# A ring of gathered rows, released by SyncE at an exact count of slots in place of a bound

## The chip, the cores and the metric

The kernel runs on one core of a Trainium2 chip. The metric is the device time of one execution in microseconds; where there are several, their median counts.

## The reference

A graph of 2500 nodes (512 features) and 40000 edges, sorted by destination, goes through two layers of attention with 8 heads of 64, and after them through a dense mixing layer, a node MLP and a gated feed-forward network. Only the attention matters here:

```python
for l in range(L):                                   # L = 2
    q, k, v = (x @ Wq[l] + bq[l]), (x @ Wk[l] + bk[l]), (x @ Wv[l] + bv[l])     # (N, H, D) each
    a = (q[dst] * k[src]).sum(-1) * scale
    e = jnp.exp(a - segment_max(a, dst)[dst])
    alpha = e / (segment_sum(e, dst)[dst] + 1e-16)
    agg = segment_sum(alpha[:, :, None] * v[src], dst)
    x = agg + (x @ Ws[l] + bs[l]) + enc
```

## The kernel before

The program is a row of stages, each in a block that ends with a barrier of all engines: ordering of the edges (skipped where they are sorted), `index_edges`, `normalise_project` (projections of the first layer), `edge_attention`, `combine_project` (projections of the second layer), `edge_attention` again, and then the dense stages. There is no scheduler: what stands in an engine's block runs in that order, and semaphores join the engines.

**Tiles and slots.** The edges lie in ET = 313 tiles of 128. The nodes lie in NT = 20 tiles of 128. Since the edges are sorted, an edge tile mostly belongs to one node tile, and where a node tile begins inside an edge tile, that edge tile is worked on twice. One such piece of work is a slot: there are USED = ET + NT - 1 = 332 of them, in the order of the edges. Edge tile t is used for the last time in slot t + (the number of later node tiles begun by then), so at most in slot t + 19.

**`index_edges`** finds out which slot belongs to what, once, for both layers. VectorE counts edges per node tile, gets from it for each node tile its first edge tile (`flo`), its first slot (`cum`) and how much slot and edge tile differ by then (`dshift`, stepwise). It puts such numbers on a diagonal (`diag`) and reduces it, so that they lie one to a partition (`begins`); compares all slot numbers with them (`begun`); and TensorE sums over the partitions by a matmul of 20x336. The results go as integers into `numbers`, 32 partitions each, from which the engines load registers: `tile_of`, `k_arrival`, `v_arrival`. The masks that follow are written to HBM by SyncE (line 443), and the stage ends with their landing.

**`edge_attention`** first computes the scores (k rows), then the softmax, then the aggregation (v rows). Both gathers go through `ring`: 48 buffers of 128x512 f32, all 48 of which serve for v. In the aggregation

- GpSimd issues one gather (indirect DMA) of 128 rows for each edge tile (line 1244). At most four are in flight: before gather n it waits for the landing of gather n - 4 (FLIGHT). It also waits until the buffer is free:

```python
else:
    pool.wait_ge(weighted, t - NV + NT + 1)
pool.sem_inc(started, 1)
gather(n, v_dram, t)
```

  Tile t takes the buffer of tile t - NV (NV = 48), and the count t - NV + NT + 1 is one that holds for it however the node tiles lie: 20 slots more than slot t - NV itself.
- SyncE waits for the landings in order and counts them for VectorE in `v_arrived` (`arrive`, line 1213):

```python
for t in range(ET):
    arrive(ET + t, v_arrived)
```

- VectorE weights the rows of each slot with the attention weights (line 1373, 128x512), which raises `weighted` by one. Before each fourth slot it builds a matrix of ones and zeros (line 1362), copies weights (1365) and loads the arrival numbers of the next four slots into registers (`slot_numbers`). It may be 16 slots ahead of TensorE.
- TensorE sums slot after slot into PSUM, two halves of a row, four f32 matmul records a slot (line 1506). ScalarE writes out each finished node tile (lines 1429 to 1432).

Of the kernel before, what the change touches and what calls it, by code (L numbers as in the profile page):

```python
# [14 lines left out]
P = 128  # L15
# [7 lines left out]
NT = -(-N // P)  # L23
NP = NT * P
LAST = N - (NT - 1) * P
ET = -(-E // P)
# [18 lines left out]
NV = 48  # L45
# [140 lines left out]
def share_edges(nc, mem, T):  # L186

    T["full_at"] = mem.sb("full_at", [P, NT], I32)
    numbers = mem.sb("numbers", [P, SLOTS], I32)
    T["tile_of"], T["k_arrival"], T["v_arrival"] = (numbers[r:r + 32, :] for r in (0, 32, 64))  # L190
    T["local"] = mem.sb("local", [P, SLOTS + U // 2])
    T["disorder"] = mem.sb("disorder", [P, 1], I32)
    T["local_rows"] = nc.dram_tensor("local_rows", (SLOTS, P), BF16).ap()
    T["src"] = mem.sb("src", [P, ET], I32)
    T["mask_rows"] = nc.dram_tensor("mask_rows", (P, MASKS), BF16).ap()
    T["linked"] = mem.sb("linked", [H, 2 * CH, 2 * CH], BF16)
# [145 lines left out]
def index_edges(nc, a, T, ordered, names):  # L342


    with ExitStack() as stack:
# [20 lines left out]
        diag = m.sb("diag", [NT, 2, NT])  # L366
        begins = m.sb("begins", [NT, 2])
        begun = m.sb("begun", [NT, SLOTS])
        step_up = m.sb("step_up", [NT, P])
# [32 lines left out]
        with nc.Block() as block:  # L402
# [46 lines left out]
            def _(vec):  # L449
# [44 lines left out]
                c.then(vec.tensor_tensor(diag[:, 1, :], dshift[0:NT, :], ident, ALU.mult))  # L494
                c.wait()
                c.then(vec.tensor_reduce(begins[:], diag[:], AX.X, ALU.add))
                c.wait()
                c.then(vec.tensor_scalar(begun[:], slot[0:NT, :], begins[:, 0:1], None, ALU.is_ge))
                c.then(vec.tensor_scalar(step_up[:], ones[0:NT, :], begins[:, 1:2], None, ALU.mult))
                c.wait()  # L500
                vec.nop().then_inc(begun_done, 1)
                vec.wait_ge(stepped, 2)
# [4 lines left out]
                for r, first in (("k_arrival", K_FIRST), ("v_arrival", V_FIRST)):  # L507
                    at = slice(32, 64) if first == K_FIRST else slice(64, 96)
                    c.then(vec.tensor_scalar(T[r], etile[at, :], float(ET - 1), float(first), ALU.min, ALU.add))
                c.then(vec.tensor_scalar(up[:], cum[:, 1:NT + 1], 1.0, None, ALU.add))  # L510
                c.wait()
                c.then(vec.tensor_copy(T["full_at"][:], up[:]))
                for k in range(EK):

                    c.then(vec.tensor_scalar(pick[:, k, :], etile[:], -float(P * k), part[:, 0:1], ALU.add,
                                             ALU.is_equal))
# [55 lines left out]
            def _(pe):  # L572
# [10 lines left out]
                pe.matmul(pss[:], step_up[:], begun[:], start=True, stop=True).then_inc(stepped, 1)  # L583
                pe.wait_ge(picked, 1)
# [555 lines left out]

def edge_attention(nc, a, T, layer, k_dram, v_dram, agg_dram, q_space, y_space, scores):


    with ExitStack() as stack:
# [4 lines left out]
        PER_ROWS = 8  # L1149
        ring = m.sb("ring", [P, NV, C])  # L1150
# [50 lines left out]
        agg_out = [m.sem(f"agg_out{b}") for b in range(AB)]  # L1201
        k_arrived, v_arrived = m.sem("k_arrived"), m.sem("v_arrived")
# [5 lines left out]
        with nc.Block() as block:  # L1208
            @block.sync
            def _(sp):  # L1210
# [22 lines left out]
                for t in range(ET):  # L1233
                    arrive(ET + t, v_arrived)

            @block.gpsimd
            def _(pool):
# [17 lines left out]
                for t in range(ET):  # L1255
                    n = ET + t
                    if t < NB:
                        pool.wait_ge(multiplied, min(n - NB + NT + 1, USED))
                    elif t < NV:

                        pool.wait_ge(reduced, BATCHES)
                        pool.wait_ge(reduced_act, BATCHES * (B - V) * H)
                    else:
                        pool.wait_ge(weighted, t - NV + NT + 1)
                    pool.sem_inc(started, 1)
                    gather(n, v_dram, t)
# [1277 lines left out]
```

## Time and profile before

| | |
|---|---|
| median of three runs | 3196.03 us |
| lowest and highest | 3192.73 and 3197.9 us |
| the profiled execution's own time | 3192.62 us |
| its span, from the first to the last instruction | 3190.5 us |
| TensorE matmul / weight load busy | 2531.2 / 1883.2 us |
| VectorE / ScalarE / GpSimd busy | 2171.0 / 1150.6 / 1644.5 us |
| mean granted TensorE clock | 0.899 of full speed |

The profiled execution is a run of its own, 0.1% below the median of the three. The busy times are sums over stages with different limits, so a share of the span says little on what a change in one stage is worth. The aggregation of the first layer runs from about 803 to 1170 us of the span, that of the second from about 1884 to 2252 us.

### The profile page before, as it was taken

The page shows a single profiled execution, that of the slowest core. Times are in us where ns is not written, and L with a number is a line of the kernel's source. Part 1 is how long each engine was busy: PE and PEld are TensorE (multiplying, and loading weights), DVE is VectorE, ACT ScalarE, POOL GpSimd, SP SyncE. Part 2 cuts the span into 40 slices and gives each one's busy share as a digit, 9 for nine tenths or more (in the row PEclk, how much of TensorE's full clock was granted, in tenths as well). Part 3 has the DMA queues.
Part 4 walks back from the last instruction along what each step waited for, and adds up shares of the span by engine and source line. Part 5 has one row for each costly group of instructions (what it writes and reads, how often), then busy time and mean ns, then how long its engine had stood idle before and what let it go on. Part 6 is the DMA issues. An engine that isn't in the chain of part 4 may idle for free. (4 is left out here: it accounts for less than half of the span.)

```text
span 3190.5 us, 46149 instructions
## 1 busy us (share of the span) xinstructions
PE 2531.2 (79%) x9872; PEld 1883.2 (59%) x9872; DVE 2171.0 (68%) x3512; ACT 1150.6 (36%) x4306; POOL 1644.5 (52%) x1559
## 2 busy tenths in 40 slices
PE   1999766664988879996666759888785999699998
PEld 1788444433776557874444448666564767477776
DVE  5766588888967765437888888777465454566665
ACT  0555466664000020016666610000353322155554
POOL 0101577777677741117777767777122443355555
PEclk9999787877999989997877769999887999899999
DMA  2565577776677774437777757777542332251111
GB/s 102 169 209 181 172 209 206 209 210 189 194 210 222 222 238 139 139 116 211 209 211 210 211 170 212 224 220 219 170 144 78 109 131 92 88 174 40 39 42 36
DMA packets 215857, 524.52 MB, mean 164 GB/s; under 512 B 30652, under 2 KB 48424, under 8 KB 215238
## 3 DMA queue, kind: packets, MB, share of 16 engines
q0 software_dynamic: 100160, 328.28, 35.5%
q1 hardware_dynamic: 98182, 161.91, 15.1%
q10 hardware_dynamic: 17280, 31.63, 2.6%
q8 instruction: 94, 1.54, 0.2%
q14 instruction: 141, 1.16, 0.1%
HBM read 439.83 MB, written 81.88 MB: 164 GB/s over the span
## 5 line engine op out<-in xcount | busy, mean ns | idle before, releaser
L1244 POOL DMA_INDIRECT edge_ring<-v_rows,edges_src x626 | 616.4, 985 | 237.3 <-issue 133.2
L1244 POOL DMA_INDIRECT edge_ring<-k_rows,edges_src x626 | 592.0, 946 | 252.9 <-issue 147.8
L1506 PE MATMUL edge_psA<-layer_q_space 128*128 128x256 f32 (+1 forms) x2656 | 639.0, 395 | 99.0 <-DVE layer_q_space L1373 90.8
L1506 PEld LDWEIGHTS edge_psA<-layer_q_space 128*128 128x128 f32 x2656 | 499.9, 194 | 237.8 <-issue 167.5
L1373 DVE TENSOR_TENSOR layer_q_space<-edge_ring,edge_psQ 128x512 f32<-128x512 f32 x664 | 431.9, 689 | 173.3 <-SPq L1213 136.8
L108 PE MATMUL proj_psP<-proj_w,proj_xT 128*128 128x512 f32 x1920 | 465.9, 400 | 7.0 <-DVE proj_xT L846 4.0
L1460 PE MATMUL edge_psQ<-layer_q_space,edge_hotT 128*128 x888 | 336.7, 527 | 132.8 <-ACT edge_hotT L1398 87.0
L1385 ACT ACTIVATE edge_ring<-edge_ring 128x64 f32<-128x64 f32 x1328 | 319.9, 242 | 286.2 <-DVE edge_ring L1296 286.2
L108 PEld LDWEIGHTS proj_psP<-proj_w,proj_xT 128*128 128x128 f32 x1920 | 359.7, 190 | 91.3 <-DVE proj_xT L846 4.4
L1296 DVE TENSOR_TENSOR edge_ring<-edge_psQ,edge_ring 128x512 f32<-128x512 f32 x444 | 286.4, 684 | 102.2 <-ACT edge_ring L1385 69.9
L1460 PEld LDWEIGHTS edge_psQ<-layer_q_space,edge_hotT 128*128 128x128 f32 x888 | 218.3, 257 | 218.6 <-issue 172.4
L1277 DVE TENSOR_REDUCE layer_scores<-edge_ring 128x24 f32<-128x1536 f32 x166 | 289.4, 1743 | 0.0
L2415 POOL TENSOR_TENSOR ffn_sums<-ffn_sums 128x512 f32<-128x512 f32 x110 | 173.0, 1573 | 199.2 <-DVE ffn_sums L2445 199.2
L1429 ACT COPY layer_q_space<-edge_psA 128x256 f32<-128x256 f32 x80 | 26.1, 379 | 688.2 <-PE edge_psA L1506 688.2
L1385 ACT ACTIVATION_READ_ACCUMULATOR edge_ring<-edge_ring 128x1 f32 x1328 | 247.6, 186 | 0.0
L1460 PE MATMUL edge_psA<-layer_q_space,edge_hotT 128*128 x440 | 169.2, 520 | 62.2 <-ACT edge_hotT L1398 39.1
L1296 DVE TENSOR_TENSOR edge_ring<-edge_psA,edge_ring 128x512 f32<-128x512 f32 x220 | 142.5, 684 | 49.1 <-ACT edge_ring L1385 37.4
L1460 PEld LDWEIGHTS edge_psA<-layer_q_space,edge_hotT 128*128 128x128 f32 x440 | 106.5, 254 | 105.2 <-issue 82.8
L2384 ACT ACTIVATE ffn_sums<-ffn_psP,kept_means 128x512 f32<-128x512 f32 x220 | 139.3, 684 | 79.7 <-PE ffn_psP L2339 78.5
L2445 DVE SCALAR_TENSOR_TENSOR ffn_sums<-ffn_psP,kept_means,ffn_sums 128x512 f32<-128x512 f32 x220 | 154.6, 743 | 17.1 <-PE ffn_psP L2339 16.6
L108 PE MATMUL ffn_psO<-ffn_downT,ffn_hT 128*128 128x512 f32 x660 | 153.2, 391 | 0.0
L1445 PE MATMUL edge_psA<-layer_y_space,edge_ones 1*128 1x512 bf16 x166 | 76.3, 462 | 90.1 <-DMA layer_y_space<-local_rows 90.0
(295 smaller groups left out, 3442.3 us busy)
## 6 DMA issues: line engine op xcount, KB each, us to landing
agg_rows<-layer_q_space ACTq DMA_DIRECT2D x40, 260.0 KB, 4.0
base_rows<-proj_enc SPq DMA_DIRECT2D x40, 256.0 KB, 2.1
k_rows<-proj_out ACTq DMA_DIRECT2D x40, 256.0 KB, 3.4
v_rows<-proj_out ACTq DMA_DIRECT2D x40, 256.0 KB, 2.5
edge_ring<-k_rows,edges_src POOLq DMA_INDIRECT x626, 3.7
edge_ring<-v_rows,edges_src POOLq DMA_INDIRECT x626, 3.7
ffn_downT<-down_rows SPq DMA_DIRECT2D x11, 512.0 KB, 10.2
proj_agg<-agg_rows SPq DMA_DIRECT2D x20, 260.0 KB, 3.1
```

The costliest lines, as they stand in the source:

```text
L108: last = pe.matmul(out, left[i], right[j], start=start and n == 0, stop=stop and n == 2)
L1244: pool.indirect_dma_start(ring[:, buffer[n], :], None, rows, bass.IndirectOffsetOnAxis(ap=T["src"][:, t:t + 1], axis=0)).then_inc(landed[b ...
L1277: vec.tensor_reduce(scores[:, j * B * H:(j * B + V) * H], prod[:, at:at + V, :].rearrange("p i (h d) -> p i h d", h=H), AX.X, ALU.add).the ...
L1296: vec.tensor_tensor(prod[:, s % (2 * B), :], psQ[s % QB][:], one(ring[:, bass.ds(arrived[i] % NB, 1), :]), ALU.mult).then_inc(multiplied, 1)
L1373: vec.tensor_tensor(wv[:, s % R, 0:C].rearrange("p (h d) -> p h d", h=H), ring[:, bass.ds(arrived[s % B] % NV, 1), :].rearrange("p o (h d) ...
L1385: act.activation(at, at, ACT.Copy, accum_out=scores[:, s * H + head:s * H + head + 1]).then_inc(reduced_act, 1)
L1445: pe.matmul(psB[j % 2], ones[:], rows_at[k % 2][0:1, at * P:at * P + B * P], start=True, stop=True).then_inc(spread, 1)
L1460: last = pe.matmul(psQ[(j * B + i) % QB][:], hotT[j % 2][:, i * P:(i + 1) * P], one(qp[:, k, bass.ds(tiles[i], 1), :]), start=(k == 1), st ...
L1506: last = pe.matmul(psA[:, bass.ds(d % 2, 1), e, 0:hi - lo].rearrange("p o w -> p (o w)"), hot[:, s % R, :], wv[:, s % R, lo:hi], start=Fal ...
L2384: act.activation(sums[:, f % 2, j, k, :], psP[k][:], ACT.Copy, scale=W["means"][:, j, f * KC + k:f * KC + k + 1]).then_inc(scaled, 1)
L2415: pool.tensor_tensor(sums[:, f % 2, j, 0, :], sums[:, f % 2, j, 0, :], sums[:, f % 2, j, 1, :], ALU.add).then_inc(summed, 1)
L2445: vec.scalar_tensor_tensor(out=half, in0=psP[k][:], scalar=W["means"][:, j, f * KC + k:f * KC + k + 1], in1=half, op0=ALU.mult, op1=ALU.ad ...
```

## The change

`index_edges` works out a fourth row of numbers, `slots_of`: for each edge tile the number of slots that must be done before its buffer is free. It needs a third diagonal (of `flo`), a second comparison (`opened`: which node tiles have begun by edge tile t), a third matmul and two more operations on VectorE. SyncE loads these numbers into registers, four at a time, waits on `weighted` for the exact count and raises `released` by one for each tile. It does so six tiles ahead of its own loop (AHEAD), between the signals to VectorE. GpSimd waits on `released` in place of `weighted`.

```diff
@@ share_edges
-    T["tile_of"], T["k_arrival"], T["v_arrival"] = (numbers[r:r + 32, :] for r in (0, 32, 64))
+    T["tile_of"], T["k_arrival"], T["v_arrival"], T["slots_of"] = (numbers[r:r + 32, :] for r in (0, 32, 64, 96))
@@ index_edges
-        diag = m.sb("diag", [NT, 2, NT])
-        begins = m.sb("begins", [NT, 2])
+        diag = m.sb("diag", [NT, 3, NT])
+        begins = m.sb("begins", [NT, 3])
...
+                c.then(vec.tensor_tensor(diag[:, 2, :], flo[0:NT, :], ident, ALU.mult))
...
+                c.then(vec.tensor_scalar(opened[:], slot[0:NT, :], begins[:, 2:3], None, ALU.is_ge))
...
-                vec.wait_ge(stepped, 2)
+                vec.wait_ge(stepped, 3)
...
+                c.then(vec.tensor_tensor(past[:], slot[:], pst[0][:, 0:SLOTS], ALU.subtract))
...
+                c.then(vec.tensor_scalar(T["slots_of"], past[96:P, :], 1.0, float(USED), ALU.add, ALU.min))
...
+                pe.matmul(pst[0][:, 0:SLOTS], step_up[:], opened[:], start=True, stop=True).then_inc(stepped, 1)
@@ new function
+def last_slots(nc, engine, T, block, n):
+
+    return nc.values_load_multi_w_load_instructions(T["slots_of"][0:1, bass.ds(block, n)], engines=[engine.engine],
+                                                    min_val=1, max_val=USED)[1]
@@ edge_attention
+        AHEAD = 6
...
+        released = m.sem("released")
...
                 for t in range(ET):
+                    r = t + AHEAD - NV
+                    if 0 <= r < ET - NV:
+                        if r % B == 0:
+                            ends_of = last_slots(nc, sp, T, r, B)
+                        sp.wait_ge(weighted, ends_of[r % B])
+                        sp.sem_inc(released, 1)
                     arrive(ET + t, v_arrived)
...
-                        pool.wait_ge(weighted, t - NV + NT + 1)
+                        pool.wait_ge(released, t - NV + 1)
```

The first place is VectorE in the indexing. Before, from the second diagonal product to the last small integer conversion:

```order
L494 TENSOR_TENSOR index_diag<-index_dshift,kept_ident 20x20
L496 TENSOR_REDUCE index_begins<-index_diag 20x2
L498 TENSOR_SCALAR index_begun<-index_slot,index_begins 20x336
L499 TENSOR_SCALAR index_step_up<-index_ones,index_begins 20x128
L503 TENSOR_SCALAR index_tile_of<-index_psd 128x336
L504 TENSOR_TENSOR index_etile<-index_slot,index_pss 128x336
L506 CAST edges_numbers<-index_tile_of 32x336
L509 TENSOR_SCALAR edges_numbers<-index_etile 32x336 x2
L510 TENSOR_SCALAR index_up<-index_cum 128x20
L512 CAST edges_full_at<-index_up 128x20
```

And with the change, at the same place (the third diagonal product, line 497 there, stands just ahead of these):

```order
L499 TENSOR_REDUCE index_begins<-index_diag 20x3
L501 TENSOR_SCALAR index_begun<-index_slot,index_begins 20x336
L502 TENSOR_SCALAR index_opened<-index_slot,index_begins 20x336
L503 TENSOR_SCALAR index_step_up<-index_ones,index_begins 20x128
L507 TENSOR_SCALAR index_tile_of<-index_psd 128x336
L508 TENSOR_TENSOR index_etile<-index_slot,index_pss 128x336
L510 CAST edges_numbers<-index_tile_of 32x336
L513 TENSOR_SCALAR edges_numbers<-index_etile 32x336 x2
L514 TENSOR_TENSOR index_past<-index_slot,index_pst 128x336
L515 TENSOR_SCALAR index_up<-index_cum 128x20
L517 CAST edges_full_at<-index_up 128x20
L518 TENSOR_SCALAR edges_numbers<-index_past 32x336
```

Four operations come in (lines 497, 502, 514 and 518), and nothing changes its order. TensorE gets one matmul of 20x336 behind the two that were there.

The second place is SyncE's queue from the score stage to the end of the first layer's attention. Semaphore instructions have no rows of their own in this listing. Before, nothing but waits and increments follows the load of the masks:

```order
L1222 DMA layer_y_space<-local_rows 1x1024 x41
L1222 DMA layer_y_space<-local_rows 1x512
L1230 DMA layer_q_space<-mask_rows 128x8066
L1208 UNCONDITIONAL_BRANCH
L978 UNCONDITIONAL_BRANCH
```

And with the change:

```order
L1237 DMA layer_y_space<-local_rows 1x1024 x41
L1237 DMA layer_y_space<-local_rows 1x512
L1245 DMA layer_q_space<-mask_rows 128x8066
L1150 TENSOR_LOAD edges_numbers
L1150 ISA x8
```

The last two rows come 67 times in each layer, once for every four of the 265 tiles from 42 on in SyncE's loop, between the waits for landings: one load from SBUF and eight register instructions. On GpSimd no instruction is added; its 265 waits for `weighted` become waits for `released`.

## Rows read from the trace of the kernel before

**Rows 1.** Busy time by engine in three stretches of the first aggregation.

```profile
804.00:854.00 50.00, 48.26 (x213) 41.65 (x214) 49.36 (x102) 0.00 (x0) 32.64 (x35) 0.95 0.63 182
854.00:877.00 23.00, 23.00 (x107) 19.95 (x106) 21.19 (x44) 1.26 (x3) 17.02 (x18) 1.00 0.74 216
877.00:1163.00 286.00, 242.32 (x985) 183.81 (x984) 203.08 (x386) 21.36 (x51) 208.87 (x221) 0.98 0.75 220
```

The columns are: from and to, length, busy us (instructions) of TensorE matmul, TensorE weight load, VectorE, ScalarE and GpSimd, then granted clock, share of the DMA engines and GB/s.

**Rows 2.** Waits of VectorE and TensorE, 877 to 1163, and VectorE at 877.

```profile
DVE layer_q_space L1373 <- SPq L1213: 67.0, 95, 2.8
...
PE edge_psA L1506 <- DVE layer_q_space L1373: 40.4, 50, 2.1
...
877.10 1.32 DVE L1373 TENSOR_TENSOR layer_q_space<-edge_ring,edge_psQ 128x512 f32<-128x512 f32 x2 [0.31 <-SPq L1213]
```

In the first two: engine, what waited, for what, us in total, times, longest. The third is a row of the timeline: start, us, engine, line, operation, how many, idle time before it and who ended it.

**Rows 3.** SyncE's waits for landings, 830 to 1167 and 804 to 805.

```profile
SPq L1213 <- DMA edge_ring<-v_rows,edges_src: 327.9, 261, 3.4
...
SPq L1213 <- DMA edge_ring<-v_rows,edges_src: 1.1, 1, 1.1
```

**Rows 4.** Timeline: gathers 47, 48, the last, 48 of layer two; VectorE's start.

```profile
813.56 0.94 POOL L1244 DMA_INDIRECT edge_ring<-v_rows,edges_src  x1 [0.30 <-issue]
821.74 0.94 POOL L1244 DMA_INDIRECT edge_ring<-v_rows,edges_src  x1 [7.24 <-DVE layer_q_space L1373]
...
1161.95 0.94 POOL L1244 DMA_INDIRECT edge_ring<-v_rows,edges_src  x1 [0.30 <-issue]
...
1903.02 0.94 POOL L1244 DMA_INDIRECT edge_ring<-v_rows,edges_src  x1 [7.23 <-DVE layer_q_space L1373]
...
803.56 0.21 DVE L1365 TENSOR_SCALAR layer_q_space<-layer_scores 128x32 f32<-128x32 f32 x1
804.64 2.48 DVE L1373 TENSOR_TENSOR layer_q_space<-edge_ring,edge_psQ 128x512 f32<-128x512 f32 x4 [0.87 <-issue]
```

**Rows 5.** Waits of GpSimd, 821 to 1163.

```profile
POOL edge_ring L1244 <- issue: 56.4, 185, 0.3
POOL edge_ring L1244 <- DVE layer_q_space L1373: 25.9, 59, 7.2
POOL edge_ring L1244 <- DMA edge_ring<-v_rows,edges_src: 15.7, 21, 2.1
```

**Rows 6.** DMA issues of the page: line, count, median us from issue to landing.

```profile
edge_ring<-v_rows,edges_src POOLq DMA_INDIRECT x626, 3.7
```

**Rows 7.** Timeline of SyncE at the end of the indexing.

```profile
66.31 0.32 SPq L443 DMA_DIRECT2D mask_rows<-layer_q_space  x1
74.87 1.29 SPq L663 DMA_DIRECT2D proj_x<-x  x3
```

**Rows 8.** Timeline of VectorE and TensorE in the indexing.

```profile
35.26 0.17 DVE L493 TENSOR_TENSOR index_diag<-index_cum,kept_ident 20x20 f32<-20x20 f32 x1
35.35 0.16 DVE L494 TENSOR_TENSOR index_diag<-index_dshift,kept_ident 20x20 f32<-20x20 f32 x1
...
35.77 0.38 DVE L498 TENSOR_SCALAR index_begun<-index_slot,index_begins 20x336 f32<-20x336 f32 x1
36.08 0.27 DVE L499 TENSOR_SCALAR index_step_up<-index_ones,index_begins 20x128 f32<-20x128 f32 x1
39.10 0.51 DVE L503 TENSOR_SCALAR index_tile_of<-index_psd 128x336 f32<-128x336 f32 x1 [2.75 <-PE index_pss L583]
39.52 0.49 DVE L504 TENSOR_TENSOR index_etile<-index_slot,index_pss 128x336 f32<-128x336 f32 x1
...
40.41 0.68 DVE L509 TENSOR_SCALAR edges_numbers<-index_etile 32x336 int32<-32x336 f32 x2
...
36.46 1.48 PE L582 MATMUL index_psd<-index_begun,index_ones 20*128 20x336 f32 x2 [3.48 <-DVEq L501]
37.74 1.32 PE L583 MATMUL index_pss<-index_begun,index_step_up 20*128 20x336 f32 x2
```

**Rows 9.** Timeline of GpSimd while VectorE works on the softmax's maxima.

```profile
793.18 1.62 POOL L1244 DMA_INDIRECT edge_ring<-v_rows,edges_src  x1 [0.30 <-issue]
```

More of the change, by code:

```diff
@@ L365, in index_edges @@
         etile = m.sb("etile", [P, SLOTS])
-        diag = m.sb("diag", [NT, 2, NT])
-        begins = m.sb("begins", [NT, 2])
+        diag = m.sb("diag", [NT, 3, NT])
+        begins = m.sb("begins", [NT, 3])
         begun = m.sb("begun", [NT, SLOTS])
+        opened = m.sb("opened", [NT, SLOTS])
+        past = m.sb("past", [P, SLOTS])
         step_up = m.sb("step_up", [NT, P])
```

## The prediction

> **What bounds the kernel now.** The kernel is a row of stages closed by barriers, and the change touches two of them: the indexing at the start and the aggregation, which runs once in each layer. So I read each from its own rows. I began with the busy times of the engines in three stretches of the first layer's aggregation [rows 1]. For the first 50 us VectorE is busy 49.36 us of 50, so it sets the pace. For the next 23 us TensorE is busy the whole time. In the last 286 us no compute engine is full: TensorE has 242.32 us and VectorE 203.08 us. Something else paces that stretch, and the waits say what it is: VectorE waits 67.0 us for SyncE (which only passes on that a gather has landed), and TensorE waits 40.4 us for VectorE [rows 2]. SyncE itself waits 327.9 us of the 337 us from 830 to 1167 for landings [rows 3]. The chain leads back to GpSimd, which issues the gathers.
>
> GpSimd needs 0.94 to 0.95 us for a gather and leaves 0.30 us before the next, whoever it waits for, so a gather starts every 1.25 us at best [rows 4]. Its idle time after 821 splits into 185 gaps put down to issue (56.4 us, 0.30 each), 59 put down to VectorE (25.9 us, the longest 7.2) and 21 to a landing (15.7 us) [rows 5]. Take 0.30 us from each: the issue gaps leave nothing, the landings leave 9.4 us, and of the VectorE gaps one is all but the whole: 59 x 0.30 + 6.94 = 24.6 of 25.9 us. That one gap is the subject of this change. Gather 47, the last that fits the ring of 48, starts at 813.56 and ends at 814.50; gather 48 starts at 821.74, after 7.24 us of idleness put down to VectorE's multiplication by the weights [rows 4]. The second layer shows the same, 7.23 us before 1903.02. The reason is the old bound: gather 48 waits for 21 slots to be weighted, though its buffer is free after slot 0. The first weighting starts at 804.64 [rows 4] and 21 of them take until about 821.5.
>
> **What the exact count takes away.** With it gather 48 needs one weighted slot, which is there at about 805.4. The other wait in front of it, the landing of gather 44, is over by about 813.5: that gather starts 3 x 1.25 us before gather 47, at 809.81, and the median from issue to landing is 3.7 us [rows 6]. So gather 48 starts at GpSimd's own pace, 0.30 us after 814.50, at 814.80. That is 6.94 us sooner in the first layer (7.24 - 0.30) and 6.93 us sooner in the second (7.23 - 0.30): **-13.87 us** for GpSimd. Later on there is nothing more to gain from the looser bound: the 1.3 us left over above is all that VectorE gaps cost beyond the usual 0.30 after the first.
>
> Does the stage end earlier by as much? The gain sits at the start of a stage in which GpSimd's chain of 265 further gathers sets the end. The ring now runs dry later (VectorE's waits for SyncE become a pattern from 877.10 on [rows 2]), because the surplus built up by then is larger. From 854 the surplus shrinks at the difference between TensorE's 0.86 us a slot (107 matmuls, four a slot, in 23.00 us [rows 1]) and 1.25 us a gather, that is by about 0.36 tiles a microsecond. Gathers that are 5.5 tiles ahead (6.94 / 1.25) put the dry point some 15 us later, near 892, still with 260 us of the stage to go. After that everything follows the landings as before, 6.9 us sooner. The limit of the idea is TensorE's idleness: it waits 40.4 us in the last stretch, so removing 6.9 us leaves more than 33 us. I take the full shift. At worst, half is given back to landings that come late in a different pattern; those cost 9.4 us per layer today.
>
> **What it adds in the indexing.** This runs once, and it is all on the path: VectorE and TensorE hand each other a chain here, the masks at its end go out at 66.31 and SyncE's next transfer, past the barrier, issues at 74.87 [rows 7]. Nothing runs beside it that is longer. By distances between starts [rows 8]:
> - the third diagonal product, 0.09 (35.26 to 35.35);
> - a second comparison over 20x336, 0.31 (35.77 to 36.08);
> - a third matmul of 20x336 before VectorE may go on, 1.28 (36.46 to 37.74), since VectorE's next instruction at 39.10 starts as the second one ends;
> - the subtraction that reads PSUM over 128x336, like the one next to it, 0.42 (39.10 to 39.52);
> - the conversion to 32x336 integers, 0.34 (two like it take 0.68 together).
> The reduction over 60 elements in place of 40 adds hundredths. The sum is **+2.44 us**. From below, if the two last operations overlapped with others in full, it is 1.7 us; from above, with each operation at its whole duration (2.7 us together) and an assumed gap of 0.2 us at four of them, 3.5 us.
>
> **What it adds on SyncE.** SyncE now has 265 waits and increments and 67 register loads of four numbers in each layer, queued in front of the signals on which VectorE waits. No row times such a load on SyncE. From the nearest rows: between the issue of VectorE's small copy and its first weighting stands just such a load, and VectorE is idle 0.87 us there [rows 4]; from below, a load that hides in the queue costs nothing. A wait with its increment costs SyncE (337 - 327.9) / 269 = 0.03 us [rows 3]. I take 0.9 us a load: with eight further waits and increments that is 1.2 us for four tiles, and four tiles take 5.00 us. The load stands between two landings that are 1.25 us apart, so it fits, just; a late signal would be caught up by VectorE, which in the last stretch is busy 203.08 of 286 us [rows 1]. SyncE has to reach gather 48's release in time as well. It is caught up by 804 to 805, where it already waits for a landing [rows 3]. The release of 48 stands behind the signal of tile 41, which starts 6 x 1.25 us before 813.56, at 806.06, and lands at about 809.8; with a load of 0.9 us the release is out at 810.7, 4 us before it is wanted. From then on the release of gather n stands behind landing n - 7, while GpSimd itself must wait for landing n - 4: three gathers, 3.75 us, are the cover. So SyncE costs **0 us**; if the cover were gone, see the third rival.
>
> **A rule against it.** While VectorE ran the maxima over masks and rows, the gather at 793.18 took 1.62 us [rows 9]; beside the weighting, with VectorE nearly full, gather 47 took 0.94 us [rows 4]. The gathers that move into 814.8 to 821.7 run beside that same weighting. The sum goes by the second row. The Trainium skill ("SBUF — State Buffer", section "SBUF: two separate sides") says that GpSimd cannot write its descriptors while VectorE runs an operation that takes both ports. By that rule, were the weighting such an operation, the moved gathers would be slower and part of the gain lost; the rows for exactly this pairing speak against it.
>
> **Sum.** -13.87 + 2.44 = -11.43 us. The profiled execution took 3192.62 us (span 3190.5), so its like would take 3181.2. It was the fastest of those shown; against the median of 3196.03 the same sum gives **3184.6 us**, 0.36% less. What a measurement can tell from no change is about 0.2%, 6.4 us.
>
> **Rivals.**
> - *The gain is given back*, because another engine turns out to bound the aggregation, and only the indexing's cost is left: 3196.0 + 2.4 = 3198.5. For it: TensorE is full from 854 to 877. Against: its 40.4 us of waiting afterwards. Or the release is not earlier, because SyncE is late at tile 42; the same time. Against: it waits for landings at 804 to 805. Together 0.10.
> - *Half is given back*, by gathers that land late more often, or by one layer only: -6.9 + 2.4 = -4.5, 3191.5. The moved gathers at 1.62 us would give much the same: six times 0.68 us, twice, is 8 us lost, 3192.8. Together 0.09.
> - *SyncE becomes the bound* (slower). Its place is the register load before each fourth tile. It decides once four tiles cost SyncE more than 5.00 us, for which a load would have to take over 4.7 us. If each of the 134 loads put its 0.87 us into the chain of gathers, that would be +117 us less 11.4, 3301. Against it stands the load's own 0.87 us. 0.04.
> - *The forecast*, both shifts whole, 0.77.
>
> **Range and chances.** The forecast's own spread is the indexing's 1.7 to 3.5 us, the landings' pattern (some 2 us each way) and that of three runs, which lay 5.2 us apart: 3179 to 3190. To leave out no more than 2 in 10 I reach to the half case: 3178.5 to 3192. Faster by over 0.2% is the forecast with a little of the half case, 0.80; within 0.2% the rest of the half case and the first rival, 0.15; slower 0.05.
>
> **What would show it.** GpSimd's gap before gather 48 should be 0.30 us in both layers, the time from the first weighting to the last gather's start 350.4 us in place of 357.3 (804.64 to 1161.95 [rows 4]), and VectorE's waits for SyncE should set in some 15 us later. In the indexing the issue of the masks should move from 66.31 to about 68.8. SyncE should wait for landings in nearly the whole aggregation still. I would be wrong if GpSimd showed long gaps put down to SyncE, if VectorE's waits for SyncE grew beyond 67 us at the same number of gathers, or if TensorE ceased to wait after 877.

## The result, and the profile after

The changed kernel takes 3179.05 us (median of 5 runs, 3175.65 to 3180.58); the kernel before took 3192.86 us beside it (median of 5, 3191.86 to 3197.9). The ratio is 0.995, with an interval of 0.9936 to 0.9964. The medians differ by 13.8 us; the ratio, which is reckoned from the single runs and not from the two medians, gives 11.5 to 20.4 us. The time lies inside the forecast range, 5.5 us below the forecast value. The larger part of that distance, 3.2 us, is the base: the forecast was set against a median of 3196.03, which was 3192.86 here. Against its own base the forecast was -11.4 us, and the medians differ by -13.8 us.

GpSimd's and VectorE's rows in the first aggregation of the changed kernel, and GpSimd's in the second, answer to [rows 4]. First the timeline (start, us, engine, line, operation, how many, idle time before it and who ended it):

```profile
814.59 0.95 POOL L1265 DMA_INDIRECT edge_ring<-v_rows,edges_src  x1 [0.30 <-issue]
815.84 0.95 POOL L1265 DMA_INDIRECT edge_ring<-v_rows,edges_src  x1 [0.30 <-issue]
...
1153.05 0.95 POOL L1265 DMA_INDIRECT edge_ring<-v_rows,edges_src  x1 [0.31 <-issue]
...
1889.71 0.95 POOL L1265 DMA_INDIRECT edge_ring<-v_rows,edges_src  x1 [0.30 <-issue]
...
806.94 2.48 DVE L1394 TENSOR_TENSOR layer_q_space<-edge_ring,edge_psQ 128x512 f32<-128x512 f32 x4 [0.89 <-issue]
...
899.17 1.97 DVE L1394 TENSOR_TENSOR layer_q_space<-edge_ring,edge_psQ 128x512 f32<-128x512 f32 x3 [0.28 <-SPq L1228]
901.82 0.69 DVE L1394 TENSOR_TENSOR layer_q_space<-edge_ring,edge_psQ 128x512 f32<-128x512 f32 x1 [0.68 <-SPq L1228]
```

Gather 48 (815.84, and 1889.71 in the second layer) now follows gather 47 after 0.30 us, in place of 7.24 and 7.23. It took 0.95 us beside the weighting, so the moved gathers were not slowed. From the first weighting to the last gather's start are 1153.05 - 806.94 = 346.1 us; the forecast was 350.4. VectorE's waits for SyncE become a pattern from 899.17 on, 92.2 us after the first weighting; before, it was from 877.10 on, 72.5 us after it. That is some 20 us later, where 15 had been forecast.

The waits of GpSimd from 815 to 1154, of SyncE from 830 to 1158, and of VectorE and TensorE from 879 to 1154 (us in total, times, longest) answer to [rows 2, 3, 5]:

```profile
POOL edge_ring L1265 <- issue: 54.5, 179, 0.3
POOL edge_ring L1265 <- SPq L1254: 29.9, 81, 1.1
POOL edge_ring L1265 <- DMA edge_ring<-v_rows,edges_src: 3.8, 6, 1.2
...
SPq L1228 <- DMA edge_ring<-v_rows,edges_src: 210.3, 195, 3.0
...
DVE layer_q_space L1394 <- SPq L1228: 60.5, 88, 2.2
...
PE edge_psA L1527 <- DVE layer_q_space L1394: 38.6, 52, 1.2
```

GpSimd's total is about what its pace of 0.30 us a gather needs: 88.2 us in 266 gaps, 8.4 more than 266 x 0.30. TensorE still waits, so it did not become the bound. One row is not as forecast: SyncE waits for landings only 210 of 328 us, where it waited 327.9 of 337 us before.

The indexing answers to [rows 7, 8]. The timeline of VectorE, TensorE (its third matmul) and SyncE:

```profile
35.32 0.17 DVE L495 TENSOR_TENSOR index_diag<-index_cum,kept_ident 20x20 f32<-20x20 f32 x1
40.70 0.51 DVE L507 TENSOR_SCALAR index_tile_of<-index_psd 128x336 f32<-128x336 f32 x1 [3.87 <-PE index_pst L590]
...
39.34 1.32 PE L590 MATMUL index_pst<-index_opened,index_step_up 20*128 20x336 f32 x2
...
68.80 0.32 SPq L445 DMA_DIRECT2D mask_rows<-layer_q_space  x1
76.41 1.29 SPq L670 DMA_DIRECT2D proj_x<-x  x3
```

The masks go out 2.49 us later (68.80 for 66.31), of which 1.54 us lie between the first diagonal product and the operation at 40.70 (5.38 us; it was 3.84) and 0.89 us behind it. But the next stage starts only 76.41 - 74.87 = 1.54 us later: from the masks' issue to it are 7.61 us in place of 8.56.

### The profile page after: what moved, and what is told of

The parts are those of the page before. It is cut to its first block and busy times, and to the rows that moved or that the text cites. A ratio compares the mean times of both kernels' runs of the same rounds, so it can differ in the third digit from the quotient of the medians.

```text
span 3178.7 us, 47893 instructions
## 1 busy us (share of the span) xinstructions
PE 2531.7 (80%) x9874; PEld 1884.4 (59%) x9874; DVE 2171.7 (68%) x3516; ACT 1150.7 (36%) x4306; POOL 1644.3 (52%) x1559
## 3 DMA queue, kind: packets, MB, share of 16 engines
q8 instruction: 94, 1.54, 0.2%
## 5 line engine op out<-in xcount | busy, mean ns | idle before, releaser
L1527 PE MATMUL edge_psA<-layer_q_space 128*128 128x256 f32 (+1 forms) x2656 | 627.2, 391 | 91.2 <-DVE layer_q_space L1394 86.5
```

What stands on the lines that cost most here:

```text
L1527: last = pe.matmul(psA[:, bass.ds(d % 2, 1), e, 0:hi - lo].rearrange("p o w -> p (o w)"), hot[:, s % R, :], wv[:, s % R, lo:hi], start=Fal ...
```

## The experiments

**The theory** is the forecast's: the exact count takes away one gap of 6.9 us at the start of each aggregation, which moves the whole chain of gathers forward, and nothing else; the indexing costs some of it, and SyncE nothing. **Rivals:** the gain comes from the looser release of the ring throughout the stage, or from SyncE standing between the engines; or SyncE does have a price, paid from the gain. The first four kernels were timed beside the kernel before at a median of 3192.49 us (26 runs). Of the others, the two with six in flight by themselves, the first with AHEAD = 2 and the last below had it at 3196.64 us beside them (17 runs), and the other four at 3195.87 us (9 runs). The ratios are against these, and are reckoned from the single runs, so they can differ a little from the quotient of two medians.

### The indexing alone

The change without SyncE's loop, and with GpSimd's old wait; the fourth row of numbers is worked out and not used.

```diff
-                        pool.wait_ge(released, t - NV + 1)
+                        pool.wait_ge(weighted, t - NV + NT + 1)
```

> The change's indexing alone: the fourth row of numbers is worked out, but SyncE loads and relays nothing and GpSimd waits for the old bound. My theory (the release gains about 13.9 us, the indexing costs 1.5 to 2.5 us): the masks go out at about 68.8 in place of 66.31, the gap before gather 48 stays at 7.2 us in both layers, and the time is 1.5 to 2.5 us above before, ratio 1.0005 to 1.0008. Rival (the indexing's shift, or the lines themselves, gives the extra 2 to 4 us that the change won beyond the forecast): the time is 2 us or more below before.

Measured: 3192.21 us (11 runs), ratio 1.0001 (0.9993 to 1.001). The masks go out at 68.51 and the next stage starts at 76.10: 1.23 us later than before. So the indexing costs no more than the interval allows, about 3 us; the expected 1.5 to 2.5 us are too little to be seen in the time, and of the rival (2 us or more below) the interval leaves only its edge, 2.2 us. The profiles say more: over all of this study the next stage starts at 74.34 to 75.15 without the new indexing (six) and at 76.03 to 76.80 with it (seven), 1.6 us from mean to mean.

### The relay over SyncE alone, with the old bound

```diff
                 for t in range(ET):
+                    r = t + 6 - NV
+                    if 0 <= r < ET - NV:
+                        sp.wait_ge(weighted, r + NT + 1)
+                        sp.sem_inc(released, 1)
                     arrive(ET + t, v_arrived)
...
-                        pool.wait_ge(weighted, t - NV + NT + 1)
+                        pool.wait_ge(released, t - NV + 1)
```

> SyncE's relay alone: SyncE waits for the old bound (a constant, no register loads) six tiles ahead and raises released, GpSimd waits for released; no new indexing. My theory (the relay costs nothing and brings nothing): the gap before gather 48 stays at 7.2 to 7.4 us, the rest of GpSimd's late starts in the aggregation stays near 10 us a layer, ratio 1.000 within 0.1%. Rival (the relay itself changes how gathers fall against the writes of the aggregate, and so brings the extra 2 to 4 us): late starts beyond the first gap fall to 7 to 9 us a layer, ratio 0.999. Second rival (the relay costs): released comes late, gaps put down to SyncE, ratio over 1.001.

Measured: 3193.43 us (12 runs), ratio 1.0005 (0.9995 to 1.0014). The gap before gather 48 is 7.26 us in both layers. The relay brings nothing, and costs nothing that can be told from the noise (4.5 us at most by the interval). Behind gather 48 GpSimd loses 9.8 and 11.1 us over its pace of 1.25 us a gather in the two layers, before 10.5 in both; so the rival, by which the relay itself brings the extra gain (7 to 9 us), did not come. SyncE's waits for landings from 830 to 1150:

```profile
SPq L1214 <- DMA edge_ring<-v_rows,edges_src: 293.9, 248, 3.9
```

In the kernel before they are 312.4 us in this stretch, so the added wait and increment take (312.4 - 293.9) / 256 tiles = 0.07 us each time.

### The exact count alone, as constants

No indexing and no relay: GpSimd waits on `weighted` for exact counts that are written into the program, right for these inputs alone.

```diff
+        BEGUN = (71, 101, 123, 143, 159, 188, 201, 212, 224, 234, 245, 255, 264, 274, 282, 291, 300, 308)
...
-                        pool.wait_ge(weighted, t - NV + NT + 1)
+                        pool.wait_ge(weighted, t - NV + 1 + sum(at <= t - NV for at in BEGUN))
```

> GpSimd waits for weighted at the exact counts, written into the program as constants that hold for these inputs only; no new indexing, no relay, no loads. My theory: the gap before gather 48 is 0.3 us in both layers and nothing is paid for it, so the time is 1.5 to 2.5 us below the change, 13 to 18 us below before, ratio 0.9945 to 0.996. Rival (the relay or the loads cost the change something in the aggregation): 4 us or more below the change. Rival (the extra gain comes by the relay): about the change's time or above, 10 to 12 us below before.

Measured: 3179.05 us (9 runs), ratio 0.9958 (0.9942 to 0.9973), and the gap before gather 48 is 0.30 us in both layers. The earlier release by itself gives the gain, about 13.4 us (8.6 to 18.5 by the interval). 1.5 to 2.5 us below the change had been expected; the median is the change's own, so what indexing and relay cost together is too little to be told apart here. Neither is a cost of 4 us or more for the relay seen.

### Nine slots more than the exact count

```diff
-                c.then(vec.tensor_scalar(T["slots_of"], past[96:P, :], 1.0, float(USED), ALU.add, ALU.min))
+                c.then(vec.tensor_scalar(T["slots_of"], past[96:P, :], 10.0, float(USED), ALU.add, ALU.min))
```

> The change with nine slots added to each exact count (the integer conversion adds 10.0 in place of 1.0). My theory (only the one gap before gather 48 mattered, because ten slots are weighted by 804.64 + 10 x 0.78 = 812.5, before gather 47 ends): the gap is 0.3 us still and the time is the change's within 0.1%. Rival (a buffer released earlier is worth something through the whole aggregation, as a deeper ring would be): about half of the gain is lost, 5 us or more above the change.

Measured: 3181.36 us (5 runs), ratio 0.9967 (0.9954 to 0.998); the interval overlaps the change's. By the ratios alone a loss of 5 us is not excluded, so the profile has to decide: the gap before gather 48 is 0.30 us in both layers, since the tenth slot is weighted at 810.71, before gather 47 starts at 812.07, and from the first weighting to the last gather are 348.9 and 350.5 us, with the exact constants 350.0 and 350.3. So exactness is worth nothing beyond that one gap: the ring is not short anywhere else.

### Six gathers in flight, and the releases nine ahead

What is left over GpSimd's pace of 1.25 us a gather in the changed kernel is 7.4 us in the first aggregation and 9.6 in the second, in gathers that start late. Here is one of them in GpSimd's timeline:

```profile
905.33 0.95 POOL L1265 DMA_INDIRECT edge_ring<-v_rows,edges_src  x1 [0.30 <-issue]
906.85 0.94 POOL L1265 DMA_INDIRECT edge_ring<-v_rows,edges_src  x1 [0.57 <-SPq L1254]
```

Such gathers mostly come 5 to 7 us behind the issue of a write of `agg_rows` (here at 900.75). The row names SyncE's release; but with the constants, where GpSimd waits for nothing from SyncE, late starts cost as much (11.1 and 10.2 us), so the release is not their cause.

```diff
-        AHEAD = 6
+        AHEAD = 9
...
-                FLIGHT = 4
+                FLIGHT = 6
```

> The changed kernel with six gathers in flight in place of four (FLIGHT = 6) and releases nine tiles ahead in place of six. Theory A: what is left over the pace of 1.25 us a gather in the aggregation, 7.4 us in the first layer and 9.6 us in the second by the profile of the changed kernel, comes from gathers that wait for a landing that is late by 1 to 2 us, and a wait for the landing of two gathers earlier stands 2.5 us behind such a landing: it goes to under 2 us a layer, the score stage gains a little as well, and the time is 3179 - 15 = 3164 us or less (0.991 of before). Rival B: the late landings are a shortage of the DMA engines, which more gathers in flight only queue up behind; the late starts stay within 2 us of 7.4 and 9.6, and the time is 3179 us. Rival C: the ring's releases then come too late, since TensorE or VectorE bounds the stage: GpSimd's gaps are put down to the release, and the time is between.

Measured: 3152.97 us (4 runs, 3152.1 to 3154.28), ratio 0.986 (0.9846 to 0.9874). GpSimd's waits from 809 to 1140:

```profile
POOL edge_ring L1265 <- issue: 64.9, 213, 0.3
POOL edge_ring L1265 <- SPq L1254: 15.9, 52, 0.3
```

No wait is longer than 0.3 us. What starts late is 0.8 us a layer, and gather 47 comes 7.2 and 6.8 us sooner after the start of its stage (its first load on SyncE's queue), since the gathers of the score stage have the same limit. Theory A holds and was too modest (26 us less than the change, where 15 were expected). That more in flight would only queue up at the DMA engines (B) is refuted, and so is a shortage of released buffers (C). Two numbers are changed here, AHEAD as well; that the gain is that of six in flight is shown by the next run and by the one with constants and six in flight, which have no releases by SyncE.

### Six in flight in the kernel before

```diff
-                FLIGHT = 4
+                FLIGHT = 6
```

> The kernel before with six gathers in flight in place of four, the bound of 20 slots more kept. Theory A, the late landings go: the gap before gather 48 stays at 7.2 us in both layers, and the gathers behind it lose under 2 us a layer in place of 10.4: 3192.5 - 17 = 3175.5 us, so the exact count is worth its 12 to 13 us still on top. Rival C: with the bound kept the ring of 48 is short by 20 slots, and GpSimd, no longer late, runs into VectorE: gaps put down to it beyond gather 48 that come to more than 3 us a layer, and the time is above 3180 us. Rival B, more in flight brings nothing: 3192.5 us.

Measured: 3171.70 us (5 runs), ratio 0.9921 (0.9907 to 0.9934). The timeline of GpSimd at gathers 47 and 48:

```profile
805.85 0.95 POOL L1244 DMA_INDIRECT edge_ring<-v_rows,edges_src  x1 [0.30 <-issue]
817.74 0.95 POOL L1244 DMA_INDIRECT edge_ring<-v_rows,edges_src  x1 [10.94 <-DVE layer_q_space L1373]
```

Now GpSimd fills the ring sooner, gather 47 only 5.2 us after the first weighting in place of 8.9, and the old bound costs 10.94 us in the first layer and 10.95 in the second. Theory A had the gap stay at 7.2 us; it was right on the late landings (0.9 and 0.8 us a layer). This is a second measurement of the mechanism, with a larger gap: the exact count should be worth (10.94 - 0.30) + (10.95 - 0.30) = 21.3 us less 1.6 for the indexing, some 20, and 3171.70 - 3152.97 = 18.7 us were measured. Behind gather 48 there is again no wait above 0.3 us, so rival C is refuted beyond the one gap.

### The releases two tiles ahead: SyncE without its cover

```diff
-        AHEAD = 6
+        AHEAD = 2
```

> The changed kernel with the releases two tiles ahead of SyncE's own loop in place of six (AHEAD = 2). The release of gather n then stands behind the landing of gather n - 3, so the cover of three gathers is gone and three are in flight in place of four. Theory A, no price for a register load: a gather every (3.7 + 0.3) / 3 = 1.33 us, 0.08 us x 265 = 22 us a layer more, some of it in place of the late landings: 3179 + 44 = 3223 us at most. Theory B, the load is on the chain once in four gathers and costs what stands before VectorE's first weighting, 0.9 us: 66 x 0.9 = 60 us a layer on top of that, up to 3340 us; each 0.1 us of a load's price is worth 13 us. Rival: fewer in flight land sooner by as much, and the time stays at 3179 us; then SyncE would have no price even without cover.

Measured: 3467.82 us (5 runs), ratio 1.0845 (1.0831 to 1.0859), 289 us more than the change. GpSimd's timeline:

```profile
883.09 0.94 POOL L1265 DMA_INDIRECT edge_ring<-v_rows,edges_src  x1 [1.74 <-SPq L1254]
884.33 0.95 POOL L1265 DMA_INDIRECT edge_ring<-v_rows,edges_src  x1 [0.30 <-issue]
885.58 0.95 POOL L1265 DMA_INDIRECT edge_ring<-v_rows,edges_src  x1 [0.30 <-issue]
887.31 0.94 POOL L1265 DMA_INDIRECT edge_ring<-v_rows,edges_src  x1 [0.78 <-SPq L1254]
890.10 0.94 POOL L1265 DMA_INDIRECT edge_ring<-v_rows,edges_src  x1 [1.85 <-SPq L1254]
```

Four gathers take 7.0 us here (883.09 to 890.10), 7.3 on average. The rival (no price without cover) is refuted, and both theories are far too low: A gave 3223 us at most, B 3340, and the time is 128 us above that. B had the loads at 120 us in the two layers; what the rest is, the next run takes apart.

### Two tiles ahead, without the register loads

The relay with exact counts as constants, right for these inputs alone.

```diff
+                    r = t + 2 - NV
+                    if 0 <= r < ET - NV:
+                        sp.wait_ge(weighted, r + 1 + sum(at <= r for at in BEGUN))
+                        sp.sem_inc(released, 1)
                     arrive(ET + t, v_arrived)
...
-                        pool.wait_ge(weighted, t - NV + NT + 1)
+                        pool.wait_ge(released, t - NV + 1)
```

> The kernel before, with SyncE's waits and increments as in the change and only two tiles ahead, but with the exact counts written as constants (for these inputs alone): no register load, no fourth row in the indexing. It has the chain of the run with AHEAD = 2 and not its loads. Theory A, the 289 us that this run lost are the loads' price: here a gather starts every 1.33 us at most (three in flight, 3.7 us from issue to landing and 0.3 us of handing over), and the time is 3179 to 3223 us. Theory B, they are the price of three in flight and of the way over SyncE: a gather starts every 1.83 us here too, and the time is about 3465 us.

Measured: 3328.70 us (5 runs), ratio 1.0424 (1.041 to 1.0438). Neither theory: half of the 289 us stay without any load. GpSimd's timeline, and its waits from 880 to 1140:

```profile
952.68 0.94 POOL L1250 DMA_INDIRECT edge_ring<-v_rows,edges_src  x1 [0.48 <-issue]
954.13 0.94 POOL L1250 DMA_INDIRECT edge_ring<-v_rows,edges_src  x1 [0.51 <-issue]
955.49 0.94 POOL L1250 DMA_INDIRECT edge_ring<-v_rows,edges_src  x1 [0.41 <-issue]
957.04 0.94 POOL L1250 DMA_INDIRECT edge_ring<-v_rows,edges_src  x1 [0.61 <-issue]
...
POOL edge_ring L1250 <- issue: 58.3, 125, 2.1
POOL edge_ring L1250 <- SPq L1239: 46.5, 41, 2.3
```

With three in flight a gather starts every 1.45 us even in a quiet stretch (952.68 to 957.04 are three), where 1.33 had been worked out, so the landing with both handings-over takes about 4.4 us and not 4.0. The mean over the layer is 1.58 us; the surplus over 1.45 is put down here to late landings, which with three in flight go straight into the chain, but no run tests that. The loads' share is the difference of the two runs: 3467.82 - 3328.70 = 139.1 us for 134 loads, **1.04 us each** in the chain (1.00 by the two ratios). It includes the 1.6 us of the new indexing, which this run does not have.

### Two tiles ahead, eight numbers to a load

```diff
-        AHEAD = 6
+        AHEAD = 2
...
-                        if r % B == 0:
-                            ends_of = last_slots(nc, sp, T, r, B)
-                        sp.wait_ge(weighted, ends_of[r % B])
+                        if r % 8 == 0:
+                            ends_of = last_slots(nc, sp, T, r, 8)
+                        sp.wait_ge(weighted, ends_of[r % 8])
```

> The changed kernel with AHEAD = 2 and eight numbers to a load in place of four, so 34 loads a layer in place of 67. Theory A, a load costs mostly once, whatever it fetches: half of what the loads cost with four numbers, 3468 - (3468 - 3200) / 2 = 3334 us. Theory B, it costs by the number: as much as with four, about 3468 us.

Measured: 3466.61 us (5 runs), ratio 1.0855 (1.0835 to 1.0876): the same as with four. The view of the load's own line, from 880 to 1140 (operation, count, shortest, median and longest in ns), first with eight numbers:

```profile
L1150 SPq FUSED_REGOPS  x144: 147/147/147, 887.6 to 1136.1; - x144
L1150 SPq SEQ_ASSERT  x144: 18/18/18, 887.8 to 1136.3; - x144
L1150 SPq TENSOR_LOAD <-edges_numbers x18: 520/524/546, 887.0 to 1133.8; - x18
```

and, from the run with AHEAD = 2 above, with four:

```profile
L1150 SPq FUSED_REGOPS  x144: 147/147/147, 881.3 to 1138.5; - x144
L1150 SPq SEQ_ASSERT  x144: 18/18/18, 881.5 to 1138.7; - x144
L1150 SPq TENSOR_LOAD <-edges_numbers x36: 294/298/1001, 880.9 to 1137.4; - x36
```

A block of four numbers is 0.298 + 4 x (0.147 + 0.018) = 0.96 us, a block of eight 0.524 + 8 x 0.165 = 1.84 us: 0.24 and 0.23 us a number. Theory B. The load's own median rises by 0.226 us for four more numbers, 0.057 us each; the larger part of the price is the register instructions behind it. The Trainium skill ("Runtime: NRT & Kernel Launch", section "Instruction fetch mechanics") gives about 200 ns a register for a register load, even in bulk. The rows show 57 ns for each further one in these loads from SBUF, so here the measurement decides.

### Three tiles ahead

```diff
-        AHEAD = 6
+        AHEAD = 3
```

> The changed kernel with AHEAD = 3: the release of gather n stands behind the landing of gather n - 4, which GpSimd waits for anyway. With AHEAD = 2 four gathers took 7.2 us on average, which is 1.25 (from one gather to the next) + 3.7 (landing) + 1.4 (a load) + 0.85 left for handing over. Theory A, by the same sum without the first term: four gathers take 5.95 us in place of 5.0, 0.95 x 66 x 2 = 125 us more than 3179, 3304 us. Theory B, the handing over is hidden here since GpSimd has its own wait: 5.1 to 5.4 us, 3192 to 3232 us. Rival: four in flight hide the load, 3179 us.

Measured: 3284.75 us (5 runs), ratio 1.0276 (1.0262 to 1.029). Four gathers take 5.96 us on average in the first layer, as theory A had it; theory A added its surplus to the change's time, in which four gathers take 5.11 and 5.14 us and not 5.0, so the time is less than its 3304 us. The hand-over is in the chain here. AHEAD = 4 and 5 were not measured; with 6 the price is gone.

### Exact counts as constants, and six in flight

```diff
-                FLIGHT = 4
+                FLIGHT = 6
...
-                        pool.wait_ge(weighted, t - NV + NT + 1)
+                        pool.wait_ge(weighted, t - NV + 1 + sum(at <= t - NV for at in BEGUN))
```

> The kernel before with GpSimd's waits at the exact counts as constants and six gathers in flight: no indexing of releases, no load and no way over SyncE. Theory A, on the chip the way over SyncE costs nothing with AHEAD = 9, and the new indexing 1.2 to 1.5 us: 3153.0 - 1.4 = 3151.6 us, which no interval tells from 3153. Theory B, SyncE's 134 loads still cost something in gathers that start late: under 3148 us.

Measured: 3147.88 us (4 runs, 3143.95 to 3150.9), ratio 0.9855 (0.984 to 0.987). No run of it is as slow as the fastest with the relay (3152.1), though the intervals of the ratios overlap. By the medians it is some 5 us less, theory B's mark; by the ratios, each against the kernel before as timed beside it, it is 1.6 us, which is theory A's. So this run does not decide between them. By the profiles, 1.6 us are the indexing and 0.7 us a layer stand between gather 48 and the last (330.1 us here, 330.8 with the relay); whether there is more stays open. It has the lowest median of all, but is only right for these inputs; of the kernels that hold for any, the change with six in flight is.

### What shortens the masks' transfer

The kernel before, with five more sums on VectorE in the indexing, which nobody reads.

```diff
+        spare = m.sb("spare", [P, 5, SLOTS])
...
                 c.then(vec.tensor_tensor(etile[:], slot[:], pss[:], ALU.add))
+                for i in range(5):
+                    c.then(vec.tensor_tensor(spare[:, i, :], slot[:], pss[:], ALU.add))
```

> The kernel before with five more subtraction-like sums of 128x336 (slot number plus PSUM) on VectorE in the indexing, written to a spare tile that nobody reads. By the row of 0.42 us each the issue of the masks moves from 66.31 to 68.4, which is the delay of the new indexing without its dependencies, matmul and writes. Theory A: the masks' transfer of 6.2 us in place of 7.1 us, seen wherever the new indexing is in, goes with the moment at which it is issued: the next stage starts 1.2 us later than before and not 2.1 us. Theory B: it goes with something that the new indexing does, and the transfer takes 7.1 us: the next stage starts 2.1 us later, at about 77.0. The time is 3193.5 to 3194.6 us, which is within what a run can tell.

Measured: 3194.26 us (12 runs), ratio 0.9994 (0.9985 to 1.0004). The timeline of SyncE, and the transfer in the view of DMA issues (KB, us from issue to landing):

```profile
67.90 0.32 SPq L444 DMA_DIRECT2D mask_rows<-layer_q_space  x1
75.50 1.29 SPq L666 DMA_DIRECT2D proj_x<-x  x3
mask_rows<-layer_q_space SPq DMA_DIRECT2D x1, 2016.5 KB, 6.2
```

The masks go out 1.59 us later (not 2.1), and the next stage starts 0.63 us later. Issued at 67.9 the transfer takes 6.2 us, as at 68.4 to 69.2 with the new indexing (seven profiles); issued at 65.8 to 66.6 it took 0.95 us longer (six profiles). Theory A: it goes with the moment and not with what the new indexing does. What happens at that moment on the chip no row shows.

## Where the prediction held, and the steps that failed

**What bounds the aggregation** held. GpSimd's chain of gathers set the end of the stage before and after, and only the gap before gather 48 mattered. This is shown three times: by the constants (as much gain without anything else), by nine slots more (nearly the same gain), and by six in flight (with a larger gap, a larger gain, in size as the gap says).

**The gap term, -13.87 us**, was seen to the hundredth at its place: 0.30 us in both layers. It was passed on whole: with nothing else changed the constants gained 13.4 us, and half of it would have been 6.9, below their interval. The rivals in which it is given back, wholly or by half, are out: TensorE still waits 38.6 us behind the changed stretch, and the moved gathers took 0.95 us, not 1.62. What the prediction names as a rule against it did not come true for this pairing of operations, as the forecast had it from the rows. From the first weighting to the last gather the second layer took 349.5 us (1879.58 to 2229.09), near the forecast's 350.4; the first took 346.1, which is 4.3 us less than forecast. Of these, 1.3 us are one gather that stood earlier against the weighting, and 3 us fewer late landings (7.4 us in place of 10.4). Neither belongs to the change: with constants the late landings cost 11.1 us in the same layer, with nine slots more 9.0.

**The step of the sum that failed is the indexing term, +2.44 us: it was mis-sized.** Up to the issue of the masks it was right (2.49 us measured). But the stage ends with their landing, and this came 0.95 us sooner behind its issue. So the term is 1.54 us in this pair of profiles and 1.6 in the mean of all, below its lower bound of 1.7, which had been worked out from VectorE's overlaps alone; the transfer at the end was taken as a constant, without a reason. With 1.6 the sum is -12.3 us, inside the measured interval of -20.4 to -11.5; the forecast's -11.43 lies just outside it. What is left between -12.3 and -13.8 no run explains. It is no more than what a stage varies: with the old bound the first weighting to the last gather took from 356.0 to 357.9 us in four kernels, and in the kernel before gather 47 came 473.4 us after the start of its stage in one layer and 470.3 in the other. Base, indexing and late landings all fell to the same side, and the time lies only 0.5 us above the lower end of the stated range: that it stayed inside is luck, that the gap was passed on is not.

**SyncE's term, 0 us**, was right for AHEAD = 6, and the price of a load nearly so: 0.96 us by its instructions and 1.04 in the chain, for 0.9 estimated. What failed beside it is the step on how SyncE can become the bound, in two statements. First, "SyncE should wait for landings in nearly the whole aggregation still": it waits 210 of 328 us. That did not even follow from the forecast's own terms: the 63 blocks of 0.96 us in this stretch are 60 us, the waits and increments of the relay 0.07 us a tile (above), 18 us, and the signals 0.03 us a tile, 8 us. These are 86 of the 118 us; for the other 32 no row accounts. Second, "it decides once four tiles cost SyncE more than 5.00 us, for which a load would have to take over 4.7 us". With AHEAD = 3 a load and its register instructions, 1 us together, already cost 106 us of kernel time (near the rival's +117). The point from which SyncE decides is not its throughput but its cover: the landing, the load and the handing over must fit between the gather released and the one that it stands behind. The forecast had this as "the cover of 3.75 us" and did not carry it into the rival.

**The base.** 3.2 of the 5.5 us between forecast and result came from setting the sum against the median of three runs. Against the profiled execution, from which its rows came, it had given 3181.2.

## What to carry to other kernels

When a ring's release count is a bound, look for the first reuse of its first buffer: there the slack of the bound is paid in full, once in each pass; later it costs nothing if the consumer has caught up. A relay over a third engine is free only with cover: count landing + register loads + hand-over against the gathers between, and test it with less cover, because its price does not show otherwise. And a limit on gathers in flight should leave room for a late landing: four in flight kept GpSimd's pace between late landings, but the late ones cost 17 us in the changed kernel's two aggregations, and some more in its scores. When that limit is loosened the ring fills sooner, and a bound on its release costs more: 10.94 us in place of 7.24 here.

## What the runs showed of the hardware

- A load of four numbers from SBUF into SyncE's registers takes 0.298 us, of eight 0.524 us, and each number 0.165 us more in register instructions. Where the next step waits for it, a block of four cost 1.04 us.
- The same transfer of 2016.5 KB took 7.1 us when issued between 65.8 and 66.6 us of the span, and 6.2 us when issued from 67.9 to 69.2, with no other transfer of data issued meanwhile. The fourteen profiles agree in this; why it is so, no row shows.
- Landings that hold a gather back, by up to 2 us, mostly come some 5 to 7 us after a write of `agg_rows` by ScalarE's queue. This is a coincidence in time; no run took the writes away.
